# A new order for the first head group of a fused Perceiver layer: K and V of a block in turn, Q late, the context loaded in quarters and halves

## The chip, the cores and the metric

One core of a Trainium2 chip runs the whole layer in one launch. The metric is device time in microseconds (us). Engines are named as in the profile: PE (TensorE, matmuls), PEld (its weight loads), DVE (VectorE), ACT (ScalarE), POOL (GpSimd), SP (SyncE, which issues all loads and stores).

## The reference

All data are fp32. With LN the normalization without weights, the kernel computes for x of 128 x 512 and a context of 2048 x 512:

```
x = x + xattn(LN(x), ctx)      # cross attention
x = x + mamba2(LN(x))          # a state-space layer, one chunk of 128
x = x + ffn(LN(x))             # one 512 x 512 matrix, dequantized from 4 bits

def xattn(q_in, ctx):                       # HQ = 32 heads of Q, HKV = 8 of K and V, 128 wide
    q = rope((q_in @ wq) as 32 heads)       # 128 x 128 each
    k = rope((ctx @ wk) as 8 heads)         # 2048 x 128 each
    v = (ctx @ wv) as 8 heads
    a = softmax(q @ k.T / sqrt(128) + mask) # 4 heads of Q share one of K and V
    return concat(a @ v) @ wo
```

The change lies in the cross attention, in the first of its eight head groups alone.

## The kernel before, in words

A head group is one head of K and V with its four heads of Q. Group 0 is written out ahead of a loop (L612 to L629 on PE); each turn of the loop computes the scores and the output of group g and projects group g + 1 in between.

fp32 products are made of three passes on PE. A tensor is split into a high part (rounded to the fast fp32r type, a copy on ACT or POOL) and a low part (the tensor minus its high part, a subtraction on DVE or POOL); `pairs` (L393) adds high x high, high x low and low x high. So every operand of PE passes through two other engines first: the context (`ctx_high` on ACT, `ctx_low` on DVE), the weights `wk` and `wv` (`split_weight` on POOL), `wq` (`wqo_hi` on ACT, `wqo_lo` on DVE in group 0 and on POOL in the loop), the normalized x (`qx_hi`, `qx_lo`), rotated K (`k_high` on ACT, `k_low` on POOL) and turned Q and V (`q_high`, `v_high` on ACT, `q_low`, `v_low` on DVE).

The 2048 context positions are four blocks of 512. `project_k_block(g, b)` and `project_v_block(g, b)` are twelve matmuls each (four slices c of the inputs, three passes), and so is `project_q`. K of a block is rotated on DVE by `k_rotate`: three products that read the PSUM bank and a rope table, then an addition of `rope_a` and `rope_b`, both in SBUF. `rope_a` has two slots; block b uses slot (b + 1) % 2, and Q's rotation uses slot 0, as blocks 1 and 3 do. `transpose_q` turns rotated Q on PE, `transpose_v_block` turns V (copied out of PSUM by `first_v_copy`). `scores` computes 4 heads x 4 blocks of tiles, each masked and maximized on DVE (`mask_scores`); a tile's bank is used again four tiles later, after its masking. The fourth tile needs the low part of K of block 3.

Each engine works through its own list in the order in which it is written, and waits on semaphores; nothing is planned at run time. Around the change the order of PE in group 0 is

```
transpose_norm(1)   # 32 turned identities, then x     turn_identity(14)
K0  Q  K1  V0  turn Q  K2  V1  V2  turn V0  K3  turn V1  V3  turn V2   # then scores(0)
```

(turned identities are transposes of a constant whose result nobody reads). On DVE: layer norm of x, `ctx_low` of block 0 in two halves with `qx_lo` between them, `wqo_lo` in two halves, `ctx_low` of block 1, Q's rotation, `ctx_low` of block 2, rotation of block 0, `q_low`, rotation of block 1, `ctx_low` of block 3, rotations of blocks 2 and 3 with `v_low` between. On POOL: constants, `norm_scale`, the split of `wk`, the split of `wv`, `k_low` of blocks 0 to 3. SP issues its loads in this order: x, wk, context block 0 in two halves, wq, block 1, Q's rope tables, K's rope tables of block 0, wv, block 2, tables 1, block 3, tables 2 and 3, mask.

Of the kernel before, what the change touches and what calls it, by code (L numbers as in the profile page):

```python
# [29 lines left out]
P = 128  # L30
# [41 lines left out]
def build(nc, x, mask, ctx_t, rope_k_cos, rope_k_sin, rope_q_cos, rope_q_sin, wk, wv, wq, wo, w_dt, w_bc,  # L72
          w_hs, w_gate, w_out, conv_w, conv_b, dt_bias, a_log, d_skip, norm_w, q_packed, q_scale, q_zero,
          q_bias, out):
    with ExitStack() as whole:
# [162 lines left out]
        last_diag_hi, last_diag_lo = wk_hi[:, :, :], wk_lo[:, :, :]  # L238
        first_v_bank = [bank[6], oq_bank, ring_a[0], bank[6]]
# [32 lines left out]
        first_ctx_in = [whole.enter_context(nc.semaphore(f"first_ctx_in{i}")) for i in range(2)]  # L272
        ctx_in = [whole.enter_context(nc.semaphore(f"ctx_in{b}")) for b in range(KB)]
# [7 lines left out]
        def _(sp):  # L281
            sp.dma_start(xres[:, :], x).then_inc(s["x_in"], 16)
            sp.dma_start(wk_raw[:, :, :], wk[0]).then_inc(s["wk_in"], 16)

            def load_context(b):
                sp.dma_start(ctx_raw[:, b, :, :], ctx_t[:, :, b * 512:(b + 1) * 512]).then_inc(ctx_in[b], 16)
# [6 lines left out]
            for i, two in enumerate(PAIRS):  # L293
                sp.dma_start(ctx_raw[:, 0, two, :], ctx_t[:, two, 0:512]).then_inc(first_ctx_in[i], 16)
# [4 lines left out]
            load_rope_k(0)  # L299
            sp.dma_start(wv_raw[:, :, :], wv[0]).then_inc(s["wv_in"], 16)  # L300
            load_context(2)
            load_rope_k(1)
            load_context(3)
            load_rope_k(2)
# [87 lines left out]
        def _(pe):  # L392
# [6 lines left out]
            def turn_identity(count, spare):  # L399

                for _ in range(count):
                    pe.transpose(spare[:, 0:P], ident[:, :], ident[:, :])  # L402

            def transpose_norm(n):
                if n < 3:
                    turn_identity((32, 26)[n - 1], bank[4])
                pe.wait_ge(s["xn_ready"], n)
                for c in range(KC):
                    last = pe.transpose(oq_bank[:, c * P:(c + 1) * P], xn[:, c * P:(c + 1) * P], ident[:, :])
                last.then_inc(s["xnT_mm"], 1)  # L410

            def first_head(g):
                return isinstance(g, int) and g == 0

            def project_k_block(g, b):

                if b == 0:
                    pe.wait_ge(s["wk_lo_ready"], g + 1)
                if not first_head(g):
                    pe.wait_ge(s["scores_masked"], HG * KB * g - KB + b + 1)  # L420
                for c in range(KC):
                    if first_head(g):

                        pe.wait_ge(s["ctx_lo_ready"], 2 * b + c // 2 + 1 if b < 3 else 7)
                    last = pairs(ring_a[b][:, :], wk_hi[:, c, :], wk_lo[:, c, :],
                                 ctx_hi[:, c, b * 512:(b + 1) * 512], ctx_lo[:, c, b * 512:(b + 1) * 512],
                                 c == 0, c == KC - 1)
                last.then_inc(s["kproj_ready"], 1)

            def project_q(g):  # L430


                if first_head(g):
                    pe.wait_ge(s["qx_lo_ready"], 1)
                for c in range(KC):
                    if first_head(g) and c == 0:
# [3 lines left out]
                    last = pairs(oq_bank[:, :], qx_hi[:, c, :], qx_lo[:, c, :], wqo_hi[:, c, :], wqo_lo[:, c, :],  # L440
                                 c == 0, c == KC - 1)
# [36 lines left out]
            def transpose_v_block(g, b):  # L478

                pe.wait_ge(s["v_copied"], KB * g + b + 1)  # L480
                if b == 0:
                    if first_head(g):
                        pe.wait_ge(s["qT_lo_ready"], 1)
                    else:
                        pe.wait_ge(s["pt_lo_ready"], KT * g)
# [140 lines left out]
            project_k_block(0, 3)  # L626
# [167 lines left out]
        def _(act):  # L794
# [94 lines left out]
            act.wait_ge(first_ctx_in[0], 16)  # L889
            ctx_high(0, PAIRS[0])  # L890
            act.wait_ge(s["xnT_mm"], 1)
            act.activation(qx_hi[:, :, :].rearrange("p c t -> p (c t)"), oq_bank[:, :], ACT.Copy)\
                .then_inc(s["qx_hi_ready"], 1)
            act.wait_ge(first_ctx_in[1], 16)
            ctx_high(0, PAIRS[1])
# [3 lines left out]
            act.wait_ge(ctx_in[1], 16)  # L899
            ctx_high(1, PAIRS[0])  # L900
            ctx_high(1, PAIRS[1])
            def first_v_copy(b):
                act.wait_ge(s["vproj_ready"], b + 1)
                act.wait_ge(s["ctx_lo_ready"], 2 * b + 2)
                act.activation(first_v[b], first_v_bank[b][:, :], ACT.Copy).then_inc(s["v_copied"], 1)

            act.wait_ge(ctx_in[2], 16)
            ctx_high(2, PAIRS[0])
            ctx_high(2, PAIRS[1])
            first_v_copy(0)  # L910
            q_high(0)
            act.wait_ge(ctx_in[3], 16)
            ctx_high(3)
            k_high(0, 0)
            k_high(0, 1)
            first_v_copy(1)
            first_v_copy(2)
            v_high(0, 0)
            k_high(0, 2)
# [138 lines left out]
        def _(dve):  # L1058
# [13 lines left out]
            def k_rotate(g, b):  # L1072
# [7 lines left out]
                if b == 1:  # L1080
                    dve.wait_ge(s["qT_mm"], g + 1)
# [10 lines left out]
            def q_rotate(g):  # L1092
                dve.wait_ge(s["qproj_ready"], g + 1)
                q = oq_bank[:, :].rearrange("p (h two d) -> p h two d", h=HG, two=2)
# [4 lines left out]
                                  oq_bank[:, :].rearrange("p (h d) -> p h d", d=DH // 2), cos, ALU.mult)  # L1099
# [161 lines left out]
            dve.wait_ge(s["x_in"], 16)  # L1261
            half_stats(1, 0)
            half_stats(1, 1)
            layer_norm(1)
# [12 lines left out]
            ctx_low(0, 1, PAIRS[0])  # L1277
            dve.wait_ge(s["qx_hi_ready"], 1)
            dve.tensor_tensor(qx_lo[:, :, :].rearrange("p c t -> p (c t)"), oq_bank[:, :],
                              qx_hi[:, :, :].rearrange("p c t -> p (c t)").bitcast(F32), ALU.subtract)\  # L1280
                .then_inc(s["qx_lo_ready"], 1)
            ctx_low(0, 2, PAIRS[1])
            for two, high, low in zip(PAIRS, ("first_wq_hi", "wq_hi_ready"), ("first_wq_lo", "wq_lo_ready")):
                dve.wait_ge(s[high], 1)
                dve.tensor_tensor(wqo_lo[:, two, :], wqo_raw[:, two, :], wqo_hi[:, two, :].bitcast(F32), ALU.subtract)\
                    .then_inc(s[low], 1)
            ctx_low(1, 3, PAIRS[0])
            ctx_low(1, 4, PAIRS[1])
            dve.wait_ge(s["tables_in"], 32)
            q_rotate(0)  # L1290
            ctx_low(2, 5, PAIRS[0])
            ctx_low(2, 6, PAIRS[1])
            first_k_rotate(0)
            q_low(0)
            first_k_rotate(1)
            ctx_low(3, 7)
            first_k_rotate(2)
            v_low(0, 0)
# [230 lines left out]
        def _(pool):  # L1529
# [15 lines left out]
            def k_low(g):  # L1545
                for b in range(KB):
# [32 lines left out]
            norm_scale(1)  # L1579
            split_wk(0)  # L1580
            split_wv(0)
            k_low(0)
# [117 lines left out]
```

## Time and profile before

| | us |
|---|---|
| median of 3 runs (705.7 to 707.18) | 705.96 |
| the profiled execution | 707.14 |
| its span, first to last instruction | 705.4 |
| PE busy in the span | 694.2 (98%) |
| DVE, ACT, POOL busy | 547.5 (78%), 391.9 (56%), 299.6 (42%) |
| first head group ends, scores(0) begin | 37.41 |
| first projection of the second group begins | 48.82 |

A busy share is of the whole span; which engine sets the pace of a stage is read in the timeline of that stage. In a timeline row the first number is the start in us from the span's start, the second the duration (for a count above one, from the first start to the last end), and a bracket at its end gives the idle time ahead of it and what ended it. The ends of matmuls are modelled, so the pitch from start to start is their cost.

### The profile page before, as it was taken

The numbers are of one execution on the slowest core, as the hardware profiler recorded it, in microseconds if no ns is written. First come the engines' busy times: TensorE is split into PE (matmuls) and PEld (weight loads), VectorE is DVE, ScalarE is ACT, GpSimd is POOL, SyncE is SP. The second block draws the span as 40 slices with busy tenths as digits, with TensorE's granted clock in tenths as the row PEclk, the third lists the DMA queues.
The fourth block names the chain that finished last, engine by engine and source line by source line (L and its number), as shares of the span: only waits on it lengthen the run. The fifth ranks groups of instructions, "written<-read, shape, count | busy, mean of one in ns | idle before, by whom it ended". The sixth has DMA issues, their size and how long they took to land. (4 is left out here: it accounts for less than half of the span.)

```text
span 705.4 us, 12247 instructions
## 1 busy us (share of the span) xinstructions
PE 694.2 (98%) x4088; PEld 592.4 (84%) x4088; DVE 547.5 (78%) x1180; ACT 391.9 (56%) x601; POOL 299.6 (42%) x151
## 2 busy tenths in 40 slices
PE   8999999999999999999999999999999999999997
PEld 7888888888888888888888888799989898999976
DVE  5988578658748857775874884867999999999984
ACT  4563454536546456454553654553867676767752
POOL 3353223404503513240450440300288887888762
PEclk9999999999999999999999999999999999999999
DMA  9602022021001202202101100781678888788710
GB/s 319 269 28 76 1 74 74 0 74 59 15 15 59 74 0 74 74 0 74 59 15 39 73 22 0 274 355 64 239 270 301 323 306 334 295 334 304 280 52 16
DMA packets 20293, 93.77 MB, mean 133 GB/s; under 512 B 2608, under 2 KB 3760, under 8 KB 11440
## 3 DMA queue, kind: packets, MB, share of 16 engines
q1 hardware_dynamic: 20272, 93.50, 36.0%
q8 instruction: 12, 0.20, 0.1%
q14 instruction: 9, 0.07, 0.0%
HBM read 93.17 MB, written 0.33 MB: 133 GB/s over the span
## 5 line engine op out<-in xcount | busy, mean ns | idle before, releaser
L1562 POOL TENSOR_TENSOR wqo_lo<-wqo_raw,wqo_hi 128x2048 fp32r<-128x2048 f32 x14 | 65.0, 4641 | 163.8 <-ACT wqo_hi L797 163.8
L1230 DVE TENSOR_TENSOR pt_lo<-bank,pt_hi 128x512 fp32r<-128x512 f32 x128 | 87.8, 690 | 48.5 <-ACT pt_hi L875 47.7
L875 ACT ACTIVATE pt_hi<-bank 128x512 fp32r<-128x512 f32 x128 | 75.8, 599 | 54.5 <-PE bank L521 48.9
L1549 POOL TENSOR_TENSOR k_lo<-rope_a,k_hi 128x512 fp32r<-128x512 f32 x32 | 42.7, 1336 | 103.9 <-ACT k_hi L815 103.9
L1595 POOL TENSOR_TENSOR w_out_lo<-w_out_sb,w_out_hi 128x2048 fp32r<-128x2048 f32 x16 | 73.4, 4588 | 21.6 <-ACT w_out_hi L986 21.6
L1138 DVE CUSTOM_DVE_ANT_0 probs<-bank,mask_sb 128x512 f32<-128x512 f32 x128 | 82.0, 685 | 0.1
L1600 POOL TENSOR_TENSOR w_gate_lo<-w_gate_sb,w_gate_hi 128x2048 fp32r<-128x2048 f32 x14 | 64.7, 4623 | 16.7 <-ACT w_gate_hi L978 16.7
L858 ACT ACTIVATE probs<-probs,neg_max 128x2048 f32<-128x2048 f32 x31 | 61.9, 2002 | 3.1 <-DVE neg_max L1128 3.1
L521 PEld LDWEIGHTS bank<-ident_r,probs_r 128*128 128x128 f32 x448 | 48.6, 139 | 15.7 <-DVE pt_lo L1230 3.3
L395 PE MATMUL bank<-pt_hi,v_hi 128*128 128x512 f32 (+1 forms) x144 | 61.0, 424 | 0.0
L655 PE MATMUL bank<-xnT,w_hs_sb 128*128 128x128 f32 x512 | 60.6, 277 | 0.0
L655 PEld LDWEIGHTS bank<-xnT,w_hs_sb 128*128 128x128 f32 x512 | 58.3, 192 | 0.0
L1442 DVE SCALAR_TENSOR_TENSOR conv<-bank,cw,conv 128x127 f32<-128x127 f32 (+2 forms) x192 | 53.7, 342 | 5.3 <-DVE conv L1442 1.8
L815 ACT ACTIVATE k_hi<-rope_a 128x512 fp32r<-128x512 f32 x32 | 20.2, 633 | 60.0 <-DVE rope_a L1089 60.0
L397 PE MATMUL bank<-pt_hi,v_lo 128*128 128x512 f32 (+1 forms) x144 | 53.6, 372 | 0.0
L396 PE MATMUL bank<-pt_lo,v_hi 128*128 128x512 f32 (+1 forms) x144 | 53.5, 372 | 0.0
L395 PE MATMUL bank<-ctx_hi,wv_hi 128*128 128x512 f32 x128 | 51.2, 400 | 0.0
L395 PE MATMUL bank<-k_hi,qT_hi 128*128 128x512 f32 x128 | 51.2, 400 | 0.0
L395 PE MATMUL bank<-ctx_hi,wk_hi 128*128 128x512 f32 x128 | 50.8, 397 | 0.0
L521 PE MATMUL bank<-ident_r,probs_r 128*128 128x128 f32 x448 | 50.3, 237 | 0.0
L397 PE MATMUL bank<-ctx_hi,wv_lo 128*128 128x512 f32 x128 | 50.1, 392 | 0.0
L397 PE MATMUL bank<-ctx_hi,wk_lo 128*128 128x512 f32 x128 | 50.1, 391 | 0.0
(210 smaller groups left out, 1746.6 us busy)
## 6 DMA issues: line engine op xcount, KB each, us to landing
w_hs_sb<-in_w_hs SPq DMA_DIRECT2D x16, 1024.0 KB, 4.9
w_out_sb<-in_w_out SPq DMA_DIRECT2D x16, 1024.0 KB, 6.3
w_gate_sb<-in_w_gate SPq DMA_DIRECT2D x16, 1024.0 KB, 4.8
wqo_raw<-in_wq SPq DMA_DIRECT2D x8, 1024.0 KB, 4.8
wqo_raw<-in_wo SPq DMA_DIRECT2D x8, 1024.0 KB, 4.8
decay<-decay_rows SPq DMA_DIRECT2D x16, 512.0 KB, 6.8
ctx_raw<-in_ctx_t SPq DMA_DIRECT2D x3, 1024.0 KB, 11.2
wk_raw<-in_wk SPq DMA_DIRECT2D x8, 256.0 KB, 2.5
```

The lines of the kernel that those rows point to most:

```text
L395: pe.matmul(dst, left_hi, right_hi, start=first, stop=False)
L397: return pe.matmul(dst, left_lo, right_hi, start=False, stop=last)
L521: last = pe.transpose(ring_b[(t + 1) % 2][:, h * P:(h + 1) * P].bitcast(F32R), probs_r[:, h, t * P:(t + 1) * P], ident_r[:, :])
L655: last = pe.matmul(dst[:, t * P:(t + 1) * P], w[:, c, t * P:(t + 1) * P], xnT[:, c, :], start=c == 0, stop=c == KC - 1)
L858: act.activation(probs[:, h, :], probs[:, h, :], ACT.Exp, bias=neg_max[:, h:h + 1], accum_out=row_sum[:, h:h + 1]).then_inc(s["probs_ready ...
L875: act.activation(pt_hi[t % 3], ring_b[(t + 1) % 2][:, :], ACT.Copy).then_inc(s["pt_hi_ready"], 1)
L1138: dve.tensor_tensor_reduce(out=probs[:, h, b * 512:(b + 1) * 512], in0=ring_a[b][:, :], in1=mask_sb[:, b * 512:(b + 1) * 512], scale=1.0, ...
L1230: dve.tensor_tensor(pt_lo[t % 3], ring_b[(t + 1) % 2][:, :], pt_hi[t % 3].bitcast(F32), ALU.subtract)\
L1442: dve.scalar_tensor_tensor(conv[:, i, t, k:], hs_bank(n, i)[:, t * P:t * P + P - k], w, conv[:, i, t, k:], ALU.mult, ALU.add).then_inc(s[" ...
L1562: pool.tensor_tensor(wqo_lo[:, :, :], wqo_raw[:, :, :], wqo_hi[:, :, :].bitcast(F32), ALU.subtract)\
L1595: pool.tensor_tensor(w_out_lo[:, i, :, :], w_out_sb[:, i, :, :], w_out_hi[:, i, :, :].bitcast(F32), ALU.subtract).then_inc(s["wout_lo_read ...
L1600: pool.tensor_tensor(w_gate_lo[:, i, :, :], w_gate_sb[:, i, :, :], w_gate_hi[:, :, :].bitcast(F32), ALU.subtract).then_inc(s["gate_lo_read ...
```

## The change

In group 0 alone:

- PE turns 20 identities ahead of everything, instead of 32 and 14, and the order becomes K0 V0 K1 V1, turn x, K2 V2, turn V0, Q, K3, turn Q, turn V1, V3, turn V2. Q and turned x get banks of ring_b instead of `oq_bank`.
- SP loads wk, block 0 in four quarters, wv, x, tables 0, block 1 in halves, tables 1, block 2 in halves, wq, tables 2, block 3 in halves, Q's tables, tables 3, mask.
- ACT and DVE split block 0 by quarters and the other blocks by halves, in a new order.
- `wqo_lo` of group 0 moves from DVE to POOL, behind `k_low` of block 0 and ahead of `k_low` of blocks 1 to 3. `norm_scale(1)` moves behind the split of `wv`.
- On DVE the rotation of block 3 follows `q_low`; Q's rotation follows `ctx_low` of block 3.

```diff
 # SP
-            sp.dma_start(xres[:, :], x).then_inc(s["x_in"], 16)
             sp.dma_start(wk_raw[:, :, :], wk[0]).then_inc(s["wk_in"], 16)
             def load_context(b):
-                sp.dma_start(ctx_raw[:, b, :, :], ctx_t[:, :, b * 512:(b + 1) * 512]).then_inc(ctx_in[b], 16)
+                for i, two in enumerate(PAIRS):
+                    sp.dma_start(ctx_raw[:, b, two, :], ctx_t[:, two, b * 512:(b + 1) * 512])\
+                        .then_inc(half_ctx_in[b][i], 16)
...
+            for c in range(KC):
+                sp.dma_start(ctx_raw[:, 0, c, :], ctx_t[:, c, 0:512]).then_inc(first_ctx_in[c], 16)
+            sp.dma_start(wv_raw[:, :, :], wv[0]).then_inc(s["wv_in"], 16)
+            sp.dma_start(xres[:, :], x).then_inc(s["x_in"], 16)
+            load_rope_k(0)
+            load_context(1)
+            load_rope_k(1)
+            load_context(2)
             sp.dma_start(wqo_raw[:, :, :], wq[0]).then_inc(s["wq_in"], 16)
-            load_context(1)
+            load_rope_k(2)
+            load_context(3)
...
 # PE
             def transpose_q(g):
                 pe.wait_ge(s["qrope_add"], g + 1)
-                if not first_head(g):
-                    pe.wait_ge(s["v_lo_ready"], KB * g - 1)
+                pe.wait_ge(s["v_lo_ready"], 1 if first_head(g) else KB * g - 1)
...
-            transpose_norm(1)
-            turn_identity(14, bank[4])
-            project_k_block(0, 0)
+            turn_identity(20, bank[4])
+            project_k_block(0, 0)
+            project_v_block(0, 0)
+            project_k_block(0, 1)
+            project_v_block(0, 1)
+            transpose_norm(1)
+            project_k_block(0, 2)
+            project_v_block(0, 2)
+            pe.wait_ge(s["qx_lo_ready"], 1)
+            transpose_v_block(0, 0)
             project_q(0)
-            project_k_block(0, 1)
-            project_v_block(0, 0)
+            project_k_block(0, 3)
             transpose_q(0)
-            project_k_block(0, 2)
-            project_v_block(0, 1)
-            project_v_block(0, 2)
-            transpose_v_block(0, 0)
-            project_k_block(0, 3)
             transpose_v_block(0, 1)
             project_v_block(0, 3)
             transpose_v_block(0, 2)
...
 # ACT, the new list
+            for c in range(KC):
+                act.wait_ge(first_ctx_in[c], 16)
+                ctx_high(0, slice(c, c + 1))
+            ctx_high_halves(1)
+            first_v_copy(0)
+            k_high(0, 0)
+            ctx_high_halves(2)
...
+            (qx_hi)  first_v_copy(1)  (wqo_hi in two halves)  k_high(0, 1)
+            ctx_high_halves(3)
+            first_v_copy(2)
+            k_high(0, 2)
+            v_high(0, 0)
             q_high(0)
...
 # DVE: in k_rotate, q_rotate and the new list
-                if b == 1:
+                if b == (3 if isinstance(g, int) and g == 0 else 1):
                     dve.wait_ge(s["qT_mm"], g + 1)
...
+                    src = first_q_bank
+                    dve.wait_ge(s["k_lo_ready"], 2)
...
+            for c in range(KC):
+                ctx_low(0, c + 1, slice(c, c + 1))
+            (statistics of x)
+            first_k_rotate(0)
+            ctx_low(1, 5, PAIRS[0])
+            ctx_low(1, 6, PAIRS[1])
+            (xn)
+            ctx_low(2, 7, PAIRS[0])
+            ctx_low(2, 8, PAIRS[1])
+            first_k_rotate(1)
+            (qx_lo)
+            first_k_rotate(2)
+            ctx_low(3, 9, PAIRS[0])
+            ctx_low(3, 10, PAIRS[1])
+            v_low(0, 0)
             dve.wait_ge(s["tables_in"], 32)
             q_rotate(0)
             q_low(0)
             first_k_rotate(3)
...
 # POOL
-            norm_scale(1)
             split_wk(0)
             split_wv(0)
-            k_low(0)
+            norm_scale(1)
+            k_low(0, range(1))
+            for two, high, low in zip(PAIRS, ("first_wq_hi", "wq_hi_ready"), ("first_wq_lo", "wq_lo_ready")):
+                pool.wait_ge(s[high], 1)
+                pool.tensor_tensor(wqo_lo[:, two, :], wqo_raw[:, two, :], wqo_hi[:, two, :].bitcast(F32), ALU.subtract)\
+                    .then_inc(s[low], 1)
+            k_low(0, range(1, KB))
```

Entries in brackets stand for the statements of that name, unchanged but for their place and, for turned x and Q, their bank.

## Rows read from the trace of the kernel before

**Rows 1.** Windows: us, busy us (x instructions) by engine, clock, DMA share

```profile
2.37:10.51 8.14, 8.14 (x51) 8.14 (x51) 3.62 (x6) 2.31 (x3) 2.70 (x4) 1.00 0.98 348
...
25.21:37.41 12.20, 12.20 (x61) 10.09 (x60) 11.74 (x16) 4.36 (x8) 5.19 (x3) 1.00 0.39 160
...
48.82:442.00 393.18, 392.94 (x2055) 321.53 (x2054) 279.04 (x561) 199.75 (x280) 119.43 (x66) 1.00 0.13 43
```

**Rows 2.** Timeline of PE: start, us, engine, line, operation, tiles, shapes, count

```profile
10.51 0.47 PE L395 MATMUL bank<-ctx_hi,wk_hi 128*128 128x512 f32 x1
...
25.21 0.39 PE L395 MATMUL bank<-ctx_hi,wv_hi 128*128 128x512 f32 x1
...
27.93 0.39 PE L395 MATMUL bank<-ctx_hi,wv_hi 128*128 128x512 f32 x1
...
37.41 0.48 PE L395 MATMUL bank<-k_hi,qT_hi 128*128 128x512 f32 x1
...
48.82 0.39 PE L395 MATMUL bank<-ctx_hi,wk_hi 128*128 128x512 f32 x1
```

**Rows 3.** Timeline of PE among the first turned identities

```profile
4.35 0.84 PE L402 MATMUL bank<-ident 128*128 128x128 f32 x3
...
4.99 0.84 PE L402 MATMUL bank<-ident 128*128 128x128 f32 x3
...
8.08 0.60 PE L402 MATMUL bank<-ident 128*128 128x128 f32 x4
```

**Rows 4.** Timeline of DVE, ACT, POOL: operations that waited for loads

```profile
3.58 0.75 DVE L1062 BATCH_NORM_STATS2 stats<-xres 128x6 f32<-128x256 f32 x2 [3.58 <-DMA xres<-in_x]
...
6.41 1.06 ACT L886 ACTIVATE ctx_hi<-ctx_raw 128x1024 fp32r<-128x1024 f32 x1 [4.33 <-DMA ctx_raw<-in_ctx_t]
...
16.20 1.58 POOL L1540 CAST wv_hi<-wv_raw 128x512 fp32r<-128x512 f32 x1 [8.67 <-DMA wv_raw<-in_wv]
...
18.81 2.01 ACT L886 ACTIVATE ctx_hi<-ctx_raw 128x1024 fp32r<-128x1024 f32 x2 [2.94 <-DMA ctx_raw<-in_ctx_t]
```

**Rows 5.** Timeline of POOL: subtractions of low parts

```profile
17.86 1.30 POOL L1542 TENSOR_TENSOR wv_lo<-wv_raw,wv_hi 128x512 fp32r<-128x512 f32 x1
...
29.07 2.61 POOL L1549 TENSOR_TENSOR k_lo<-rope_a,k_hi 128x512 fp32r<-128x512 f32 x1 [2.00 <-ACT k_hi L815]
...
43.23 4.66 POOL L1562 TENSOR_TENSOR wqo_lo<-wqo_raw,wqo_hi 128x2048 fp32r<-128x2048 f32 x1 [2.31 <-ACT wqo_hi L797]
```

**Rows 6.** Timeline of DVE in the first head group

```profile
14.95 2.36 DVE L1268 TENSOR_TENSOR ctx_lo<-ctx_raw,ctx_hi 128x1024 fp32r<-128x1024 f32 x2 [0.62 <-ACT ctx_hi L886]
...
17.23 0.68 DVE L1098 TENSOR_TENSOR rope_a<-bank,cos_q 128x512 f32<-128x512 f32 x1
...
18.61 1.10 DVE L1103 TENSOR_TENSOR rope_a<-rope_a,rope_b 128x512 f32<-128x512 f32 x1
...
22.18 0.68 DVE L1084 TENSOR_TENSOR rope_a<-bank,cos_k 128x512 f32<-128x512 f32 x1
...
24.31 0.69 DVE L1089 TENSOR_TENSOR rope_a<-rope_a,rope_b 128x512 f32<-128x512 f32 x1
...
28.25 2.28 DVE L1268 TENSOR_TENSOR ctx_lo<-ctx_raw,ctx_hi 128x2048 fp32r<-128x2048 f32 x1
...
39.23 0.68 DVE L1138 CUSTOM_DVE_ANT_0 probs<-bank,mask_sb 128x512 f32<-128x512 f32 x1
```

**Rows 7.** One line's instructions: ns min/median/max, first and last start us

```profile
L1103 DVE TENSOR_TENSOR rope_a<-rope_a,rope_b x8: 1099/1225/1226, 18.6 to 403.8; 128x512 f32<-128x512 f32 x8
```

**Rows 8.** Timeline of POOL and DVE, late in the kernel

```profile
671.54 0.20 POOL L1606 TENSOR_TENSOR ms<-square_sum 128x1 f32<-128x1 f32 x1
...
688.48 2.49 DVE L1419 TENSOR_TENSOR weights<-weights,scale_sb 128x512 f32<-128x512 f32 x4
...
689.40 0.42 POOL L1606 TENSOR_TENSOR ms<-square_sum 128x1 f32<-128x1 f32 x1 [0.87 <-ACT squares L1026]
```

**Rows 9.** Timeline of ACT: one copy of the first group

```profile
36.98 0.63 ACT L815 ACTIVATE k_hi<-rope_a 128x512 fp32r<-128x512 f32 x1 [1.88 <-DVE rope_a L1089]
```

More of the change, by code:

```diff
@@ L238, in build @@
         last_diag_hi, last_diag_lo = wk_hi[:, :, :], wk_lo[:, :, :]
+        first_q_bank, first_xnT_bank = ring_b[1], ring_b[0]
         first_v_bank = [bank[6], oq_bank, ring_a[0], bank[6]]
@@ L271, in build @@
         s = {n: whole.enter_context(nc.semaphore(n)) for n in names}
-        first_ctx_in = [whole.enter_context(nc.semaphore(f"first_ctx_in{i}")) for i in range(2)]
-        ctx_in = [whole.enter_context(nc.semaphore(f"ctx_in{b}")) for b in range(KB)]
+        first_ctx_in = [whole.enter_context(nc.semaphore(f"first_ctx_in{i}")) for i in range(KC)]
+        second_ctx_in = [whole.enter_context(nc.semaphore(f"second_ctx_in{i}")) for i in range(2)]
+        third_ctx_in = [whole.enter_context(nc.semaphore(f"third_ctx_in{i}")) for i in range(2)]
+        fourth_ctx_in = [whole.enter_context(nc.semaphore(f"fourth_ctx_in{i}")) for i in range(2)]
+        half_ctx_in = [None, second_ctx_in, third_ctx_in, fourth_ctx_in]
         rope_k_in = [whole.enter_context(nc.semaphore(f"rope_k_in{b}")) for b in range(KB)]
@@ L404, in transpose_norm @@
             def transpose_norm(n):
-                if n < 3:
-                    turn_identity((32, 26)[n - 1], bank[4])
+                if n == 2:
+                    turn_identity(26, bank[4])
                 pe.wait_ge(s["xn_ready"], n)
                 for c in range(KC):
-                    last = pe.transpose(oq_bank[:, c * P:(c + 1) * P], xn[:, c * P:(c + 1) * P], ident[:, :])
+                    dst = first_xnT_bank if n == 1 else oq_bank
+                    last = pe.transpose(dst[:, c * P:(c + 1) * P], xn[:, c * P:(c + 1) * P], ident[:, :])
                 last.then_inc(s["xnT_mm"], 1)
@@ L439, in project_q @@
                         pe.wait_ge(s["wq_lo_ready"], g + 1)
-                    last = pairs(oq_bank[:, :], qx_hi[:, c, :], qx_lo[:, c, :], wqo_hi[:, c, :], wqo_lo[:, c, :],
+                    last = pairs((first_q_bank if first_head(g) else oq_bank)[:, :], qx_hi[:, c, :], qx_lo[:, c, :], wqo_hi[:, c, :], wqo_lo[:, c, :],
                                  c == 0, c == KC - 1)
@@ L480, in transpose_v_block @@
                 pe.wait_ge(s["v_copied"], KB * g + b + 1)
-                if b == 0:
-                    if first_head(g):
+                if first_head(g):
+                    if b == 2:
                         pe.wait_ge(s["qT_lo_ready"], 1)
-                    else:
-                        pe.wait_ge(s["pt_lo_ready"], KT * g)
+                elif b == 0:
+                    pe.wait_ge(s["pt_lo_ready"], KT * g)
                 if b >= 2:
@@ L887, in ctx_high, with first_v_copy, ctx_high_halves @@
                     .then_inc(s["ctx_hi_ready"], 1)
-            act.wait_ge(first_ctx_in[0], 16)
-            ctx_high(0, PAIRS[0])
+            def first_v_copy(b):
+                act.wait_ge(s["vproj_ready"], b + 1)
+                act.wait_ge(s["ctx_lo_ready"], 2 * b + 4)
+                act.activation(first_v[b], first_v_bank[b][:, :], ACT.Copy).then_inc(s["v_copied"], 1)
+            def ctx_high_halves(b):
+                for i, two in enumerate(PAIRS):
+                    act.wait_ge(half_ctx_in[b][i], 16)
+                    ctx_high(b, two)
+            for c in range(KC):
[5 more added lines that the diff above has]
+            ctx_high_halves(2)
             act.wait_ge(s["xnT_mm"], 1)
-            act.activation(qx_hi[:, :, :].rearrange("p c t -> p (c t)"), oq_bank[:, :], ACT.Copy)\
+            act.activation(qx_hi[:, :, :].rearrange("p c t -> p (c t)"), first_xnT_bank[:, :], ACT.Copy)\
                 .then_inc(s["qx_hi_ready"], 1)
-            act.wait_ge(first_ctx_in[1], 16)
-            ctx_high(0, PAIRS[1])
+            first_v_copy(1)
             act.wait_ge(s["wq_in"], 16)
@@ L1093, in q_rotate @@
                 dve.wait_ge(s["qproj_ready"], g + 1)
-                q = oq_bank[:, :].rearrange("p (h two d) -> p h two d", h=HG, two=2)
+                src = oq_bank
+                if isinstance(g, int) and g == 0:
+                    src = first_q_bank
+                    dve.wait_ge(s["k_lo_ready"], 2)
+                q = src[:, :].rearrange("p (h two d) -> p h two d", h=HG, two=2)
                 qb = rope_b[:, 0, :].rearrange("p (h two d) -> p h two d", h=HG, two=2)
@@ L1274, in first_k_rotate @@
                 k_rotate(0, b)
-            ctx_low(0, 1, PAIRS[0])
+            for c in range(KC):
+                ctx_low(0, c + 1, slice(c, c + 1))
+            dve.wait_ge(s["x_in"], 16)
+            half_stats(1, 0)
+            half_stats(1, 1)
+            dve.wait_ge(s["norm_stats"], 2)
+            dve.bn_aggr(mean_var[:, :], stats[:, :, :].rearrange("p a b -> p (a b)")).then_inc(s["norm_agg"], 1)
+            first_k_rotate(0)
+            ctx_low(1, 5, PAIRS[0])
+            ctx_low(1, 6, PAIRS[1])
+            dve.wait_ge(s["norm_rstd"], 1)
+            dve.tensor_scalar(xn[:, :], xres[:, :], mean_var[:, 0:1], rstd[:, 0:1], ALU.subtract, ALU.mult)\
+                .then_inc(s["xn_ready"], 1)
+            ctx_low(2, 7, PAIRS[0])
+            ctx_low(2, 8, PAIRS[1])
+            first_k_rotate(1)
             dve.wait_ge(s["qx_hi_ready"], 1)
-            dve.tensor_tensor(qx_lo[:, :, :].rearrange("p c t -> p (c t)"), oq_bank[:, :],
+            dve.tensor_tensor(qx_lo[:, :, :].rearrange("p c t -> p (c t)"), first_xnT_bank[:, :],
                               qx_hi[:, :, :].rearrange("p c t -> p (c t)").bitcast(F32), ALU.subtract)\
                 .then_inc(s["qx_lo_ready"], 1)
[L1282 to L1288, printed above, removed]
+            first_k_rotate(2)
+            ctx_low(3, 9, PAIRS[0])
+            ctx_low(3, 10, PAIRS[1])
+            v_low(0, 0)
             dve.wait_ge(s["tables_in"], 32)
             q_rotate(0)
-            ctx_low(2, 5, PAIRS[0])
-            ctx_low(2, 6, PAIRS[1])
-            first_k_rotate(0)
             q_low(0)
[L1295 to L1298, printed above, removed]
             first_k_rotate(3)
@@ L1543, in split_weight, with k_low @@
                     .then_inc(lo_done, 1)
-            def k_low(g):
-                for b in range(KB):
+            def k_low(g, blocks=range(KB)):
+                for b in blocks:
                     blk = slice(b * 512, (b + 1) * 512)
```

36 lines of the change are left out of this document (3 added, 33 removed).

## The prediction

> **What bounds the kernel now.** The windows come first [rows 1]: from 48.82 us on TensorE is busy 392.94 of 393.18 us. The loop therefore absorbs nothing, and whatever the first head group gains or loses until the first matmul of the second group (48.82) moves the end by as much. Next is TensorE's timeline [rows 2]: the first useful matmul starts at 10.51; from there to 37.41, where the scores begin, it hardly stands still (the second half of it shows 12.20 of 12.20 us busy [rows 1]). Twelve matmuls (one projected block) take 27.93 - 25.21 = 2.72 us. From 25.21 to 37.41 run four blocks (10.9) and three turns of V, leaving 0.44 for each turn. So the group costs TensorE about 26 us of full work, and only the 8.1 us ahead of it, filled with turned identities, can be saved there.
>
> Two more limits show. VectorE is loaded almost as densely: in the 12.20 us before the scores it works 11.74. And VectorE and GpSimd get in each other's way. In [rows 4] the GpSimd copy wv_hi takes 1.58 us, and k_lo, normally 1.30, takes 2.61 [rows 5], each while a ctx_lo runs on VectorE [rows 6]: 28.25 + 2.28 = 30.53, and k_lo ends 1.15 after that. In the other direction, the addition at 18.61 starts while wv_lo runs (17.86 + 1.30 = 19.16) and ends at 19.71. That addition needs 1.10 to 1.23 us in all eight groups [rows 7], where an addition of this size that meets nobody takes 0.69. The reader is to see that a VectorE operation with both inputs in SBUF and a GpSimd operation on SBUF exclude each other for their whole length; operations that read PSUM are spared.
>
> **The change, part by part.** Times are those of the profiled execution: 705.4 us span, 707.14 with what lies around it, 1.2 above the median of 705.96.
>
> *Loads.* All arrive on one line: 1.0 MB at 6.41, 4.3 MB at 16.20, 5.3 MB at 18.81 [rows 4], or 2.88 us per MB, whatever the size of a piece (wv is 0.25 MB, context blocks 1 MB). The bytes stay, only the order changes, and five issues are added on SP's queue; I cost those at nothing, because later loads wait for bytes and not for issues. By their place on the line: wk 3.6, the quarters 4.5 to 7.1, wv 7.9, x 8.6, rope tables of block 0 at 10.0, halves of block 1 at 11.5 and 12.9, of block 2 at 15.8 and 17.2, wq 20.1, halves of block 3 at 23.0 and 24.4. The next group's wq now leaves after the late Q; it is needed after the scores only, so nothing.
> Splitting could cost instead: the first load took 3.58 us for 0.25 MB, so at most 2.9 do not go with bytes; five pieces more give 0 to 14.5 us at the last half. I take 0, because wv lies on the line. The Trainium skill (DMA: Bandwidth & Descriptors, Bandwidth) asks for transfers of 1 MiB or more for 75% of peak, and its section on the anatomy of a DMA gives each some 2.0 us fixed; an estimate by that is 10 us later for five more pieces in a row. This trace does not agree, by wv's place on the line; as a mechanism it is rival C.
>
> *TensorE's start.* Twenty turns instead of 46, at 0.213 us each (4.35 to 4.99 holds three [rows 3]), end at 6.7. By 8.1 the turns come twice as fast (four in 0.60), after 5.7 us of unbroken turning, though the granted clock reads 1.00 throughout [rows 1, 3]: I read them as the two levels, 1.2 and 2.4 GHz. K of block 0 thus runs its first three matmuls at half pace, 6.7 to 10.1 (with early clock 9.4, with late clock 10.8). V 0 needs wv_lo: the copy of wv waits for the fourth ctx_lo to end (8.6), 0.6 and 1.3 us follow: 10.6. V 0 ends at 13.4. K 1 needs ctx_lo of block 1, behind the first rotation on VectorE (10.3, after K 0, to 13.1; 2.8 us [rows 6]): 14.4. From there K 1, V 1, the turns of x, K 2, V 2 run without a wait to 25.8: 4 x 2.74 and 0.44. Six blocks are done then; before, five were done at 25.21. What is left (Q, K 3, V 3, four turns) takes 9.6, so the scores could begin at 35.4 instead of 37.41: 2.0 us saved if nothing is late.
>
> *What is late.* wqo_lo moves from VectorE to GpSimd. 2048 columns take GpSimd 4.66 us [rows 5], so each half 2.4. Both start after ScalarE's copies: turned x at 20.5, two copies of 0.6, then wq_hi, half of 2.01 [rows 4] each: GpSimd is occupied from 22.6 to 25.0 and 25.0 to 27.4. VectorE begins the rotation of block 2 when K 2 is done (23.2). Its three products read PSUM and pass; its addition comes at 25.3 and waits till 27.4 (+2.1), done 28.1. Meanwhile k_lo of block 1, held up behind wqo_lo, stands ready and takes the port next: 28.1 to 29.4. Then ctx_lo of block 3's first half, 29.4 to 30.6; k_lo of block 2, 30.6 to 31.9; the second half, 31.9 to 33.1. K 3's second half starts at 33.1 and K 3 ends at 34.5, 3.0 after the 31.5 of a run without waits. That a waiting GpSimd operation gets in between two VectorE operations in a row is what the end of the kernel shows: while four multiplications of 0.61 follow each other on VectorE without a gap, the tiny sum ms at 689.40 takes 0.42 instead of 0.20 [rows 8] and ends 0.1 after a border with two of the four still to come.
>
> *The tail.* Q late means that block 3's rotation now stands behind Q's whole way. v_low 33.0; Q's rotation 33.6 to 35.7 (1.38 to its addition, 0.69 more [rows 6]); TensorE turns Q to 36.2, ScalarE copies (0.6) to 36.9, q_low to 37.6, rotation of block 3 to 40.3, k_hi 0.63 [rows 9] to 41.0, k_lo 1.30 to 42.4. Only then can the fourth score tile start, which used to follow the first (37.41) by three tiles of 0.68. ScalarE next copies V 3 and the high part of V 2 (42.0), VectorE's v_low of block 2 ends at 42.7, and the first masking starts there; before at 39.23 [rows 6]. Masking now sets the pace: five pieces and a v_low at 0.61 [rows 8] to 46.4, which frees the ninth tile; eight tiles of 0.68 follow: 51.9, against 48.82.
>
> **Sum.** +3.1 us: 710.2 on the profiled execution, 709.1 on the median. From late or early clock and loads 0.5 us off the line: 2.5 to 4.9 on top.
>
> **Rivals.** A, *VectorE keeps the port* for its operations in a row, and k_lo waits: the addition still loses 2.1, but ctx_lo 3 is done at 30.5, Q's rotation at 33.9, the first masking at 40.9; the same count gives 50.1, +1.3 or 707.3. For it: operations overlap by 0.08 at their borders. Against: ms [rows 8].
> B, *not slower*: the two halves of wqo_lo do not meet VectorE. The place is the addition of block 2 at 25.3; its price is 2.1 there and 2.5 behind it; the point is whether GpSimd is done or idle then. The scores start at 35.4, but Q's way (turn 31.6, masking at 38.5) leaves masking only 0.7 earlier than before: 47.7, -1.1, or 704.9. For it: the edit frees VectorE of 2.4 us. Against: both engines' work is dense, so moving either by 1 us only makes another pair meet.
> C, *each piece pays its fixed part*: the last half at 38.7, its ctx_lo at 41.1 instead of 33.1: +11, 717. Against: wv lies on the line.
>
> **How the numbers follow.** Forecast 0.63 (708.4 to 710.9), A 0.15, B 0.18, C 0.04. A difference of 0.2%, 1.4 us, is about what can be told from none: below 704.6 is faster, above 707.4 slower. Faster: under half of B, 0.08. Same: the rest of B and half of A, 0.18. Slower: the forecast, half of A and C, 0.74. The range 704.9 to 711.2 leaves out C, the forecast's top and B's lower half, together under 2 in 10.
>
> **What would show it.** Right: the first K at 6.5 to 7.0 with its first matmuls at twice the pitch; wqo_lo's halves on GpSimd between 22 and 28; an addition of block 2's rotation that lasts 2 to 3 us instead of 0.69; ctx_lo of block 3 and k_lo in turn; TensorE waiting 3 to 5 us in all between Q and the scores; first masking at 42 to 43. Wrong: that addition at 0.69, or ctx_lo of block 3 done before 29 (B); long ctx_lo waits for loads ahead of K 1 (C); a TensorE that works at half pace again after one of its waits; or a loop that regains the loss.

## The result and the profile after

Seven executions of each: before 706.75 us in the median, after 710.25, or 709.6 for the six that are compared (one, at a mean granted clock of 0.754, took 837.79 us and is left out). The ratio of the compared ones is 1.0044, 95% interval [1.003, 1.0059], so after is 3.1 us slower (2.1 to 4.2). The forecast was 709.1, or 3.1 above the median it started from. The profiled execution took 712.59, with a span of 710.6.

TensorE's waits first: in before it has none between 10 and 55 us; in after this view (engine, tile, line that waits, releaser: us in all, times, longest) shows 5.9 us of them.

```profile
PE bank L401 <- DVE ctx_lo L1274: 3.7, 3, 2.1
PE bank L455 <- DVE rope_a L1113: 0.9, 1, 0.9
PE bank L401 <- POOL wv_lo L1553: 0.9, 1, 0.9
PE bank L401 <- POOL k_lo L1560: 0.4, 1, 0.4
```

TensorE's timeline of after, answering [rows 2]: first K, V 0, K 1, V 1, turned x, the two halves of K 3, the first and the fourth score tile, the next group.

```profile
6.44 0.47 PE L401 MATMUL bank<-ctx_hi,wk_hi 128*128 128x512 f32 x1
...
10.31 0.50 PE L401 MATMUL bank<-ctx_hi,wv_hi 128*128 128x512 f32 x1 [0.86 <-POOL wv_lo L1553]
...
15.40 0.50 PE L401 MATMUL bank<-ctx_hi,wk_hi 128*128 128x512 f32 x1 [2.08 <-DVE ctx_lo L1274]
...
17.17 0.63 PE L401 MATMUL bank<-ctx_hi,wk_hi 128*128 128x512 f32 x1
17.59 0.63 PE L402 MATMUL bank<-ctx_lo,wk_hi 128*128 128x512 f32 x1
...
22.58 0.60 PE L416 MATMUL bank<-ident,xn 128*128 128x128 f32 x4
...
32.95 0.50 PE L401 MATMUL bank<-ctx_hi,wk_hi 128*128 128x512 f32 x1 [1.06 <-DVE ctx_lo L1274]
...
35.17 0.50 PE L401 MATMUL bank<-ctx_hi,wk_hi 128*128 128x512 f32 x1 [0.55 <-DVE ctx_lo L1274]
...
41.70 0.47 PE L401 MATMUL bank<-k_hi,qT_hi 128*128 128x512 f32 x1
...
44.46 0.50 PE L401 MATMUL bank<-k_hi,qT_hi 128*128 128x512 f32 x1 [0.45 <-POOL k_lo L1560]
...
54.01 0.39 PE L401 MATMUL bank<-ctx_hi,wk_hi 128*128 128x512 f32 x1
```

The second group starts 5.19 us later than in before, and the span is 5.2 longer: nothing behind the first group gives anything back, as [rows 1] had it. Of the 5.19, 1.6 are a thing of this execution: at 17.17 the matmuls stand 0.42 apart instead of 0.23. The windows show it (stretch, its length, busy us of PE, PEld, DVE, ACT and POOL, granted clock, DMA share, GB/s). Their first row shows how much less the loads moved at first (353 GB/s in the same stretch of before), and the row of ScalarE below them when the first half of context block 1 was there:

```profile
4.00:11.00 7.00, 6.14 (x29) 5.11 (x28) 4.38 (x8) 2.52 (x4) 4.51 (x6) 1.00 0.92 284
16.50:18.00 1.50, 1.50 (x5) 1.13 (x4) 1.50 (x2) 0.91 (x1) 1.32 (x1) 0.52 1.10 431
18.00:20.00 2.00, 2.00 (x6) 1.61 (x5) 1.83 (x3) 1.22 (x2) 0.00 (x0) 0.51 0.97 396
20.00:23.00 3.00, 3.00 (x17) 2.47 (x16) 2.94 (x5) 0.00 (x0) 0.00 (x0) 1.00 1.03 381
```

```profile
13.03 1.06 ACT L893 ACTIVATE ctx_hi<-ctx_raw 128x1024 fp32r<-128x1024 f32 x1 [5.32 <-DMA ctx_raw<-in_ctx_t]
```

GpSimd and VectorE, answering [rows 5] and [rows 6]: wqo_lo's second half and k_lo; then the addition of block 2, ctx_lo of block 3, q_low, the first masking.

```profile
27.69 2.40 POOL L1596 TENSOR_TENSOR wqo_lo<-wqo_raw,wqo_hi 128x1024 fp32r<-128x1024 f32 x1
30.04 1.76 POOL L1560 TENSOR_TENSOR k_lo<-rope_a,k_hi 128x512 fp32r<-128x512 f32 x1
...
43.12 1.28 POOL L1560 TENSOR_TENSOR k_lo<-rope_a,k_hi 128x512 fp32r<-128x512 f32 x1 [9.09 <-ACT k_hi L822]
```

```profile
28.15 2.49 DVE L1095 TENSOR_TENSOR rope_a<-rope_a,rope_b 128x512 f32<-128x512 f32 x1
30.57 2.33 DVE L1274 TENSOR_TENSOR ctx_lo<-ctx_raw,ctx_hi 128x1024 fp32r<-128x1024 f32 x1
...
38.96 0.69 DVE L1118 TENSOR_TENSOR qT_lo<-bank,qT_hi 128x512 fp32r<-128x512 f32 x1 [1.25 <-ACT qT_hi L817]
...
44.66 0.68 DVE L1148 CUSTOM_DVE_ANT_0 probs<-bank,mask_sb 128x512 f32<-128x512 f32 x1
```

The addition, 0.69 us when alone, ends 0.55 after wqo_lo's second half (30.09). Then the two engines change places at every operation: k_lo to 31.80, half of ctx_lo to 32.90, k_lo, the other half. Q itself, from 28.85 on, runs on TensorE without a wait, so the loss is no wait for wqo_lo.

### The profile page after: what moved, and what is told of

It is laid out like the page before. It is cut to its first block and busy times, and to the rows that moved or that the text cites. A ratio compares the mean times of both kernels' runs of the same rounds, so it can differ in the third digit from the quotient of the medians.

```text
span 710.6 us, 12208 instructions
## 1 busy us (share of the span) xinstructions
PE 693.6 (98%) x4062; PEld 589.7 (83%) x4062; DVE 550.5 (77%) x1181; ACT 392.5 (55%) x604; POOL 303.9 (43%) x153
## 3 DMA queue, kind: packets, MB, share of 16 engines
q1 hardware_dynamic: 20352, 93.50, 35.7%
## 5 line engine op out<-in xcount | busy, mean ns | idle before, releaser
L402 PE MATMUL bank<-ctx_lo,wk_hi 128*128 128x512 f32 x128 | 50.6, 395 | 0.0
```

Of the source, the lines that this page charges most:

```text
L402: pe.matmul(dst, left_hi, right_lo, start=False, stop=False)
```

## The experiments

Theory 1: the loss is GpSimd's wqo_lo and k_lo against VectorE's addition and ctx_lo. Theory 2: it is the chain behind the late Q. Theory 3: it is TensorE's clock, at 0.50 behind its waits. The table gives the ratio to before, what it makes of 707 us, and of the profiled execution the first masking and the start of the second group. In the code shown, the semaphore increments at the ends of lines are left out, and `...` marks other cuts.

| run | ratio [95%] | us to before | masking | 2nd group |
|---|---|---|---|---|
| before | 1 | | 39.23 | 48.82 |
| after | 1.0044 [1.003, 1.0059] | +3.1 | 44.66 | 54.01 |
| fill | 0.9998 [0.9986, 1.001] | -0.1 | 39.89 | 49.27 |
| sub on VectorE | 1.0031 [1.0018, 1.0045] | +2.2 | 42.12 | 51.50 |
| Q's own place | 1.003 [1.0016, 1.0045] | +2.1 | 41.00 | 50.85 |
| before, sub on GpSimd | 1.0028 [1.0017, 1.0038] | +2.0 | 41.86 | 51.45 |
| whole loads | 1.007 [1.0056, 1.0084] | +4.9 | 46.41 | 55.77 |
| addition from PSUM | 1.002 [1.0011, 1.0029] | +1.4 | 41.71 | 51.12 |
| own place and fill | 0.9986 [0.9977, 0.9996] | -1.0 | 38.63 | 48.43 |
| own place, fp32 Q | 0.9995 [0.9983, 1.0006] | -0.4 | 38.38 | 48.28 |
| whole loads, turns | 1.0061 [1.0042, 1.008] | +4.3 | 44.66 | 54.01 |
| context first | 0.9998 [0.9987, 1.0009] | -0.1 | 39.41 | 49.26 |
| and wv in halves | 0.999 [0.9979, 1.0001] | -0.7 | 38.80 | 48.60 |
| and ports apart | 0.996 [0.9946, 0.9974] | -2.8 | 36.87 | 46.78 |

In every profiled execution the rest of the span behind the second group's start is 656.5 to 656.8 us at a mean granted clock of 0.995 or 0.998, and 655.1 to 655.3 at 1.0 (the difference is one stretch at half clock between 440 and 480 us, in before as well). So the last column carries the whole effect, but of one execution: those of before at a clock of 1.0 have spans from 703.5 to 706.4, so small differences rest on the ratios. After's three executions at 1.0 have spans of 706.9 to 707.1: less 655.2, their second group starts at 51.8.

**Fill.**

```diff
-                pool.tensor_tensor(wqo_lo[:, two, :], wqo_raw[:, two, :], wqo_hi[:, two, :].bitcast(F32), ALU.subtract)
+                pool.memset(wqo_lo[:, two, :].bitcast(F32), 0.0)
```

> The kernel after, in which GpSimd fills the low half of wq of the first head group with zeros instead of subtracting (this leaves the low part of wq out of the first group's Q). A fill reads nothing from SBUF. Theory 1 (VectorE and GpSimd exclude each other while both read SBUF, and the 2 x 2.4 us of the subtraction push back rotation 2 and the splits of context block 3): rotation 2's addition takes about 0.7 us instead of 2.49, the halves of ctx_lo 3 about 1.2 to 1.3 us each instead of 2.3, the scores end 2.8 us earlier than after, and the time is about 2.8 us below after's, within 1 us of before. Theory 2 (the loss is the chain behind the late Q: turn of Q, q_hi, q_low, rotation 3, k_lo 3): the additions get short all the same, but the first masking keeps its place behind Q's rotation and the time falls by less than 0.8 us. Theory 3 (only TensorE's lower granted clock between 16.6 and 19.9 us in some executions): no change of the median by more than 0.5 us.

The loss is gone: -3.2 us against after. VectorE's timeline of this kernel: the addition takes 0.86, ctx_lo of block 3 3.44 instead of 4.55 (it still meets one k_lo).

```profile
26.11 0.86 DVE L1095 TENSOR_TENSOR rope_a<-rope_a,rope_b 128x512 f32<-128x512 f32 x1
26.90 3.44 DVE L1274 TENSOR_TENSOR ctx_lo<-ctx_raw,ctx_hi 128x1024 fp32r<-128x1024 f32 x2
```

Theory 1 holds for most of the loss, and nothing of the median is left for theory 3.

**Sub on VectorE.** The two subtractions stand ahead of qx_lo on VectorE (`dve.` for `pool.`).

> The kernel after, in which the two subtractions for the low half of wq of the first group go back from GpSimd to VectorE, ahead of qx_lo. Theory 1: the two halves take about 1.2 us each on VectorE, where they stood for 2.4 us on GpSimd; rotation 2's addition is short, the k_lo of blocks 1 and 2 still meets the ctx_lo of block 3; about 1.0 us below after's time, some 2.3 above before. Theory 2: no change (-0.3 to +0.3), as Q is still late. A third view, that VectorE's own work is what bounds this stretch: 1 to 2.5 us above after's time, as VectorE gets 2.4 us more to do.

-0.9 against after, as theory 1 said; the two intervals overlap, so the sign is not shown by the times alone. The two halves take 2.36 us on VectorE, the addition behind them 0.69. The kernel is 2.3 us above the fill: what the other engine's operation cost, VectorE's own work now costs. The operation was expensive on either engine.

**Q's own place.** Q is rotated in tiles of its own, so its rotation no longer waits for the second k_lo, nor block 3's rotation for Q's turn.

```diff
+                    src, ra, rb = first_q_bank, q_a[:, :], q_b[:, :]
...
+            first_k_rotate(3)
             q_low(0)
-            first_k_rotate(3)
```

> The kernel after, in which Q of the first group is rotated in a place of its own (SBUF that the probabilities' tiles use later), so that Q's rotation need not wait for k_lo 1, nor block 3's rotation for Q's turn; block 3's rotation then goes ahead of q_low. Theory 2 (serial chain behind Q): first masking about 1.1 us earlier, time about 1.1 below after's. Theory 1 alone (what is late is K3, by the port): VectorE gets to block 3's rotation when K3 and Q's addition are there, and the time falls by less than 0.3 us. Theory 3: 0.

-1.0: about what theory 2 said, again with overlapping intervals; the run that adds it to the fill settles it below. The addition still takes 2.49 here.

**Before, sub on GpSimd.** One edit of the change alone, in the old order.

> The kernel before with one thing of the change alone: the two subtractions for the low half of wq of the first group go from VectorE to GpSimd, behind the split of wk and ahead of that of wv. Theory 1: VectorE loses 2.4 us of work, but its splits of context block 1 and GpSimd's subtractions now stand in each other's way and wv's split is later; about 1.9 us above before's time (1.0 to 2.5). The rival, that moving work off VectorE is free or a gain: the same time as before or up to 1 us below.

+2.0, as expected. TensorE, which did not wait in before, waits twice, here for wqo_lo itself, since Q stands early in this order:

```profile
15.51 0.47 PE L395 MATMUL bank<-wqo_hi,qx_hi 128*128 128x512 f32 x1 [1.57 <-POOL wqo_lo L1579]
...
17.77 0.50 PE L395 MATMUL bank<-wqo_hi,qx_hi 128*128 128x512 f32 x1 [0.62 <-POOL wqo_lo L1579]
```

**Whole loads.**

```diff
-                for i, two in enumerate(PAIRS):
-                    sp.dma_start(ctx_raw[:, b, two, :], ctx_t[:, two, b * 512:(b + 1) * 512])
+                sp.dma_start(ctx_raw[:, b, :, :], ctx_t[:, :, b * 512:(b + 1) * 512])
```

> The kernel after with context blocks 1, 2 and 3 loaded whole again (three loads of 1 MB in place of six halves). If each piece of a load costs a fixed part (rival C), the loads behind land earlier by that part and the time falls by 1 us or more. If the loads stand on one line per byte, as the prediction had it, splitting costs nothing and what is lost is the half block of head start: the first split of each block starts 1.3 us later, K1 starts about 1 us later, and the time is 0.5 to 1.3 us above after's.

Slower by 1.8, more than expected: K 1 starts at 17.19 after a wait of 3.35, and three of six executions have a mean clock of 0.995. The one execution at a clock of 1.0 has a span of 708.4, against after's 706.9 to 707.1.

```profile
17.19 0.67 PE L399 MATMUL bank<-ctx_hi,wk_hi 128*128 128x512 f32 x1 [3.35 <-DVE ctx_lo L1272]
```

Here ScalarE splits block 1 from 14.82 on; in after it split the first half from 13.03 and the second from 14.38. So splitting these blocks pays, and rival C falls for the halves. The Trainium skill (DMA: Bandwidth & Descriptors, Bandwidth) asks for 1 MiB or more in a transfer, with figures for loads that GpSimd issues; here, where SyncE issues them, the measurement decides for 0.5 MB.

**Addition from PSUM.** The cosine product comes last and in place, so that the addition reads PSUM and SBUF.

```diff
+                dve.tensor_tensor(ring_a[b][:, :], ring_a[b][:, :], cos_k[:, blk], ALU.mult)
-                dve.tensor_tensor(rope_a[:, slot, :], rope_a[:, slot, :], rope_b[:, slot, :], ALU.add)
+                dve.tensor_tensor(rope_a[:, slot, :], ring_a[b][:, :], rope_b[:, slot, :], ALU.add)
```

> The kernel after, in which the first group's block rotations do the cosine product last and in place in PSUM, so that the addition reads one operand from PSUM and one from SBUF instead of two from SBUF. If the exclusion goes by two SBUF operands on VectorE, rotation 2's addition runs beside GpSimd's wqo_lo and takes about 0.75 us instead of 2.49; the split of context block 3 behind it still reads two SBUF operands and takes over the waiting (up to 1.9 us), so that the time falls by only 0.2 to 0.8 us. If any VectorE operand in SBUF is enough for the exclusion, the addition still takes about 2.4 us and the time does not change. If the wait were for data (semaphores) and not for the port, likewise.

The addition passes in the middle of wqo_lo (GpSimd's row, 23.93 to 28.71), and ctx_lo takes over the waiting. VectorE's timeline, then GpSimd's:

```profile
26.78 0.69 DVE L1098 TENSOR_TENSOR rope_a<-bank,rope_b 128x512 f32<-128x512 f32 x1
27.39 4.63 DVE L1285 TENSOR_TENSOR ctx_lo<-ctx_raw,ctx_hi 128x1024 fp32r<-128x1024 f32 x2
...
23.93 4.78 POOL L1607 TENSOR_TENSOR wqo_lo<-wqo_raw,wqo_hi 128x1024 fp32r<-128x1024 f32 x2 [5.91 <-ACT wqo_hi L919]
```

So it is the operands and no semaphore. By the times -1.7, more than the expected 0.2 to 0.8. From the end of wqo_lo (28.71) to the end of ctx_lo (32.02) it takes 3.3 us where after took 5.0: with the addition out of the way, the first half of ctx_lo follows wqo_lo at once, and one k_lo less stands ahead of it. That is the 1.7. The Trainium skill (GPSIMD Engine Reference, Key points) names VectorE instructions with two SBUF inputs, and those in a 2-port performance mode, as what contends with GpSimd; this trace agrees with the first.

**Own place and fill.** Both edits.

> The kernel after with both edits of the earlier runs: GpSimd fills the low half of the first group's wq with zeros (left out of Q), and Q is rotated in a place of its own with block 3's rotation ahead of q_low. If the port and the chain behind the late Q are the two parts of the loss and add up, the last score tile of the group ends at about 48.1 us (49.04 with the fill, less the 0.9 that the own place gave), and the time is 0.3 to 0.6 us below before's. If they are the same loss seen twice, it stays with the fill's, equal to before.

They add up: 4.1 below after, and 1.0 below before, though without wqo_lo's work, which before has on VectorE (2.35 us). So these two things account for the whole loss and for some 1.0 more.

**Own place, fp32 Q.**

```diff
+                    for c in range(KC):
+                        last = pe.matmul(first_q_bank[:, :], q_x[:, c, :], wqo_raw[:, c, :], start=c == 0, stop=c == KC - 1)
```

> A version meant to keep the whole computation: the kernel after with Q's place of its own, and with the first group's Q projected from unsplit float32 tiles (four float32 matmuls of 512 columns instead of twelve of the split tiles), so that neither high nor low part of the first wq is made: GpSimd loses 4.8 us and ScalarE 1.4 us of work in this stretch. What a float32 matmul of 512 columns costs no row shows; by the float32 turns (0.107 us for 128 columns at full pace) it would be 0.43 each, by four passes of the split ones' 0.23 it would be 0.92, against 0.69 for the three that it replaces: Q's projection takes 1.0 us less or 0.9 more. With the port free as with the fill, the time is between 1.5 below before's and 0.6 above; I take the dearer price and expect about the same as before (+0.3). If the port was not the cause, about 2 us above before's.

```profile
26.50 3.60 PE L453 MATMUL bank<-wqo_raw,q_x 128*128 128x512 f32 x8
...
29.51 0.59 PE L453 MATMUL bank<-wqo_raw,q_x 128*128 128x512 f32 x1
```

The trace has two records for each of the four float32 matmuls. The eighth starts 3.01 after the first, so a record costs 0.43 by the starts, a matmul 0.86 and the four 3.44. The twelve of "own place and fill" took 2.88 (26.95 to 29.83): 0.6 more on TensorE, and no wqo_lo anywhere. By the ratio the kernel is level with before, and it leaves nothing of the computation out.

**Whole loads, turns.** Whole loads again, with 6 turned identities ahead of V 0 and 28 ahead of K 1.

> The kernel with whole context loads (K1 waited 3.35 us for its first split there, and half of its executions had a mean granted clock of 0.995 instead of 0.998 or 1.0), with turned identities put into TensorE's two waits: 6 ahead of V0 and 28 ahead of K1. If the granted clock of 0.50 behind these waits comes from TensorE standing still in them, no execution is at 0.995, the granted clock is 1.00 from 10 to 23 us, and the median is about 1.7 us below that kernel's (711.3); K1 itself starts no earlier. If the clock falls for another reason (power, the neighbouring loads), half of the executions stay at 0.995 and the median within 0.5 of 713.

None of six executions is at 0.995, and the median fell from 713.01 to 711.41, as expected. By the ratios to before it is 0.6 only, and their intervals overlap; at a clock of 1.0 its four executions span 708.2 to 709.7, no less than the 708.4 of whole loads. So the times show no gain apart from the executions at 0.995, and six against six are too few to show that the turns did away with those. The waits are filled (28 turns), K 1 starts no earlier, and K 1 and V 1 take 22.59 - 17.01 = 5.58 us at full clock, where after's took 22.58 - 15.40 = 7.18: the 1.6 of its profiled execution.

```profile
13.45 3.22 PE L406 MATMUL bank<-ident 128*128 128x128 f32 x28
17.01 0.50 PE L399 MATMUL bank<-ctx_hi,wk_hi 128*128 128x512 f32 x1 [0.34 <-DVE ctx_lo L1274]
...
22.59 0.60 PE L414 MATMUL bank<-ident,xn 128*128 128x128 f32 x4
```

**Context first; and wv in halves.** The fp32 version with context block 1 loaded and split ahead of x and the first tables, block 2 ahead of the second tables; then with wv_lo in two pieces.

> The version with Q in its own place and projected in float32, and with context block 1 loaded ahead of x and the first rotation's tables, context block 2 ahead of the second's, VectorE's order to match. In that version TensorE waited 0.85 us for wv_lo and 0.62 for ctx_lo 1, and from K1 on hardly at all. If TensorE is now what bounds the group, K1 starts about 0.6 us earlier and so does all behind it: 0.6 us below that version, 0.9 below before (ratio about 0.9988). If another queue bounds it (block 0's rotation, 2.9 us later; xn), the gain is lost again and the time is that version's, or up to 1 us above it.

> The same, with the low half of the first wv made in two pieces, so that V0 starts behind the first (0.65 us earlier). If TensorE bounds the group all the way: another 0.5 us less, 1.4 below before (ratio about 0.998). If K1 waits for ctx_lo 1 in any case, the wait behind V0 grows by as much and the time is the same as without the pieces.

The first missed: K 1 came earlier, but K 2 now waited 1.23 for ctx_lo of block 2. The second brought its 0.6, by the ratios (whose intervals overlap) and by the second group's start. Why K 2 waits shows on ScalarE in the second kernel: k_hi stands ahead of the two splits, whose data had landed (they follow without a gap, and in the next kernel they begin at 14.78).

```profile
17.03 0.63 ACT L841 ACTIVATE k_hi<-rope_a 128x512 fp32r<-128x512 f32 x1 [3.19 <-DVE rope_a L1113]
17.56 1.99 ACT L912 ACTIVATE ctx_hi<-ctx_raw 128x1024 fp32r<-128x1024 f32 x2
```

**And ports apart.** Against the kernel before it: ScalarE splits block 2 ahead of k_hi, and GpSimd waits with two k_lo until VectorE's ctx_lo is done.

```diff
-            k_high(0, 0)
             ctx_high_halves(2)
+            k_high(0, 0)
...
+            pool.wait_ge(s["ctx_lo_ready"], 8)
             k_low(0, range(1))
-            k_low(0, range(1, KB))
+            k_low(0, range(1, 2))
+            pool.wait_ge(s["ctx_lo_ready"], 10)
+            k_low(0, range(2, KB))
```

> The last version with the two places mended where its trace still shows a wait: ScalarE splits context block 2 ahead of k_hi 0 (VectorE stood 1.19 us there and K2 1.08), and GpSimd waits with k_lo 0 until context block 2 is split and with k_lo 2 until block 3 is (ctx_lo 3 took 3.43 us beside k_lo 2, against 2.36 alone). If the two engines' excluding each other and ScalarE's order are what is left, K2 starts without a wait, ctx_lo 3 takes 2.4 us, the first masking comes about 1.4 us earlier (37.4 against 38.80), the last score tile at about 47.0 (48.59 in before), and the time is 1.3 to 1.6 us below before's (ratio about 0.998). If VectorE's own work bounds the group by then, half of it: 0.7 us below before's.

-2.8 to before by the ratio, -2.0 by the second group's start in the profiled executions; more than expected by either. GpSimd now waits for VectorE (the bracket in its row), K 2's wait of about 1.1 is gone from TensorE's, and ctx_lo of block 3 takes 2.35 (timelines of VectorE, GpSimd and TensorE):

```profile
26.03 2.35 DVE L1291 TENSOR_TENSOR ctx_lo<-ctx_raw,ctx_hi 128x1024 fp32r<-128x1024 f32 x2
...
28.46 1.30 POOL L1577 TENSOR_TENSOR k_lo<-rope_a,k_hi 128x512 fp32r<-128x512 f32 x1 [3.64 <-DVE ctx_lo L1291]
...
46.78 0.39 PE L411 MATMUL bank<-ctx_hi,wk_hi 128*128 128x512 f32 x1
```

This version is faster than both kernels, by 0.4% [0.26%, 0.54%] than before. What each of its two edits brings was not measured apart.

## Why the prediction was right, and where it was off

*The loop gives nothing back:* right, shown by the constant rest behind the second group in all fourteen kernels.

*Loads on one line, splitting free:* mis-sized. The first half of block 1 was split from 13.03, 1.5 later than the 11.5 at which it was forecast to land, and K 1 started at 15.40 instead of 14.4 (14.6 to 15.6 in the runs with the same start). From 4 to 11 us the queue moved 284 GB/s, in before 353: 0.48 MB less, or 1.4 us at that rate. Whether the quarters of block 0 or wv among them slow the line no run separates. Splitting the later blocks is a gain, not a price.

*TensorE's start:* K 0 at 6.44, V 0 at 10.31 (forecast 6.7, 10.6). The first three matmuls at half pace did not show in after's execution (0.31, then 0.23 apart); in the fill's they stood up to 0.57 apart. This varies from execution to execution and decides nothing, since V 0 waits for wv_lo anyway.

*The clock:* not forecast. TensorE at half pace again after a wait was listed as what would make the forecast wrong; it came, in one of after's six compared executions, and cost 1.6 there. After's three executions at 1.0 have spans of 706.9 to 707.1 without it, above all of before's at 1.0.

*wqo_lo on GpSimd against the addition, then the engines in turn:* right, in order and size. The addition lost 1.8 (forecast 2.1). From the end of wqo_lo to the end of ctx_lo it took 5.0 (forecast 5.7), as each half went through in some 1.1. Rival A (VectorE keeps the port) fell: k_lo went between the addition and the first half, and again between the two halves. Rival B's condition, no meeting, was made by the fill: equal to before rather than the 1.1 gained, for ctx_lo still met k_lo and the first masking came at 39.89, not 38.5.

*The tail behind Q:* right. From the end of ctx_lo to the first masking 9.5 (forecast 9.6), from there to the second group 9.35 (9.2). TensorE's waits between Q and the scores, forecast at 3 to 5 us, came to 2.5 (1.06, 0.55 and 0.92).

One sum of the prediction is off: three projections and four turns, at its 2.72 and 0.44, are 9.9 and not 9.6, so the scores could have begun at 35.7; the forecast time does not use it.

So the sum held: the second group starts at 51.8 in the executions at full clock and at 52.4 in the profiled one less the 1.6, forecast 51.9. The mechanism was right; that the total is right to 0.1 is luck, with the loads 1 us worse and the turn-taking 0.7 better than worked out. The share of Q's slot, which the prediction gave only as part of the tail, is about 0.9 (1.0 alone, 0.9 on top of the fill); wqo_lo on GpSimd makes 3.2. Without both, and without wqo_lo's work, the order is 1.0 ahead of before.

## What to carry to other kernels

Before moving an elementwise operation from VectorE to a GpSimd that looks idle, list what VectorE does in that stretch, operation by operation with its operands: here 4.8 us of GpSimd work cost 3 us of time, and in the last version making GpSimd wait, so that the operation on the path goes first, together with one exchange on ScalarE gave back 2. An earlier start is worth only what the last link keeps: look for the place that everything behind it waits for (here the one that Q's rotation shares with blocks 1 and 3), and give the late value one of its own.

## What was not expected of the hardware

TensorE's granted clock fell to 0.50 (16.9 to 19.5 us), the 1.2 GHz level, after waits of 0.86 and 2.08 us within 6 us, and read 1.00 again from 20 on. The two profiled executions with a mean clock of 0.995, after's and that of whole loads, both show such a stretch behind K 1's wait. A mean of 0.995 came in 1 of 6 executions with a wait of about 2 ahead of K 1, in 3 of 6 with 3.35, in 3 of 70 with 0.6 to 1.8 (the fill, sub on VectorE, own place, addition from PSUM, own place and fill, fp32 Q), and in none of six when turned identities filled the waits. That the waits are the cause is likely by these counts, and not shown.

One SBUF tensor is enough in one case: xn, a subtraction and product with two columns, takes 0.54 us alone and 1.53 beside k_lo (1.51 in after); the first row is of "context first", the next two, of VectorE and GpSimd, are of "own place and fill".

```profile
17.54 0.54 DVE L1309 TENSOR_SCALAR xn<-xres,mean_var,rstd 128x512 f32<-128x512 f32 x1
```

```profile
16.18 1.53 DVE L1301 TENSOR_SCALAR xn<-xres,mean_var,rstd 128x512 f32<-128x512 f32 x1
...
16.08 1.34 POOL L1567 TENSOR_TENSOR k_lo<-rope_a,k_hi 128x512 fp32r<-128x512 f32 x1 [4.57 <-ACT k_hi L830]
```
